# First feed-forward of a two-layer transformer kernel: the inner layers by seven products of quarters instead of eight

## The reference, cut to what matters

```python
x = L0_attn_x                                            # (4, 1024, 256)
x = x + _L0_attn_ref(_layernorm(x), Wq, Wkv_down, Wk_up, Wv_up, Wo)      # 8 heads of 64
x = x + _L0_ffn_ref(_layernorm(x), w1_w, w1_s, w2_w, w2_s, h1_w, h1_s, h2_w, h2_s, w3_w, w3_s)
x = x + _L1_attn_ref(_layernorm(x), wq, wk, wv, wo)      # 16 heads of 16, rotary
x = x + _L1_ffn_ref(_layernorm(x), w_gate, w_up, w_down) # integer weights

def _L0_ffn_ref(x, ...):                                 # the part that is changed
    def _tlin(x, w, s):  return jnp.einsum('bsi,oi->bso', x, w) * s      # w is -1, 0 or 1
    h = silu(_tlin(x, w1_w, w1_s)) * _tlin(x, w2_w, w2_s)                # 256 -> 1024, gate and up
    h = gelu(_tlin(h, h1_w, h1_s))                                       # 1024 -> 1024
    h = gelu(_tlin(h, h2_w, h2_s))                                       # 1024 -> 1024
    return _tlin(h, w3_w, w3_s)                                          # 1024 -> 256
```

## Time and profile before

| | |
|---|---|
| Median of three executions | 2337.16 us (2336.05 to 2341.58) |
| The profiled execution, its own time | 2332.85 us |
| Its span, first to last instruction | 2331.0 us |
| TensorE busy | 2286.6 us, 98% |
| VectorE, ScalarE, GpSimd busy | 1378.5, 1463.2, 1001.8 us |
| Mean granted TensorE clock | 0.996 |

### The profile page before, as it was taken

How to read it: one execution, slowest core, us unless ns; L and a number is a source line. 1 busy time by engine, 2 the same in 40 slices (tenths; PEclk the granted TensorE clock), 3 DMA queues, 4 the chain that set the end, 5 groups by cost and what they waited for, 6 DMA issues and landing times.

```text
span 2331.0 us, 39372 instructions
## 1 busy us (share of the span) xinstructions
PE 2286.6 (98%) x14921; PEld 1414.8 (61%) x14921; DVE 1378.5 (59%) x2150; ACT 1463.2 (63%) x2049; POOL 1001.8 (43%) x646
## 2 busy tenths in 40 slices
PE   7999999999998999999999999999999999999999
PEld 5455555555556888888888886444444444444688
DVE  6655766666743143232232224889889889998364
ACT  5777777777764444444444443678777777778643
POOL 2676766757763373664655645120100000000354
PEclk9999999999999999999999999999999999999999
DMA  2213222222214455555555546343332332331232
GB/s 63 69 52 100 82 74 84 82 80 76 74 31 165 158 178 183 183 182 192 182 175 190 193 165 190 92 105 77 90 87 59 93 82 64 92 90 41 81 112 77
DMA packets 156841, 259.07 MB, mean 111 GB/s; under 512 B 37004, under 2 KB 97292, under 8 KB 156300
## 3 DMA queue, kind: packets, MB, share of 16 engines
q1 hardware_dynamic: 156652, 256.53, 36.6%
HBM read 206.52 MB, written 60.68 MB: 115 GB/s over the span
## 4 chain that ended last, share of the span: by engine, by line
PE 63%; ACT 2%; DVE 1%; issue 1%; DMA 1%; SPq 1%; POOL 0%; POOLq 0%
PE m_R L130 47%; PE m_O L130 11%; PE m_X L130 4%; ACT m_P L1813 1%; DMA m_K<-bounce_k 1%; PE m_X L227 1%; SPq L1671 0%; DVE m_mraw L1965 0%; ACT m_OS L1820 0%; PE m_X L2179 0%; DVE m_ln_x L206 0%; PE m_R L227 0%; DMA inverses<-m_rinv 0%; DVE m_ln_stat L184 0%; SPq L1698 0%
## 5 line engine op out<-in xcount | busy, mean ns | idle before, releaser
L1965 DVE TENSOR_REDUCE m_mraw<-m_R 128x2 f32<-128x1024 f32 x512 | 622.6, 1221 | 68.5 <-PE m_R L130 56.0
L1813 ACT ACTIVATE m_P<-m_R 128x1024 f32<-128x1024 f32 x512 | 523.7, 1025 | 148.6 <-PE m_R L130 148.3
L130 PE MATMUL m_O<-m_P,m_V 128*17 128x256 f32 x4096 | 329.4, 393 | 4.4 <-ACT m_P L1813 2.5
L785 DVE CUSTOM_DVE_ANT_0 a_excess<-a_X,a_excess 128x512 f32<-128x512 f32 x256 | 166.5, 688 | 170.6 <-PE a_X L130 167.9
L955 POOL TENSOR_TENSOR a_accp<-a_accp,a_P 128x1024 f32<-128x1024 f32 x96 | 253.9, 2645 | 24.5 <-ACT a_P L631 16.2
L631 ACT ACTIVATE a_P<-a_S 128x1024 f32<-128x1024 f32 x256 | 249.7, 1040 | 8.5 <-PE a_S L130 8.5
L2070 POOL TENSOR_TENSOR m_act0l<-m_xf,m_act0h 128x512 fp32r<-128x512 f32 x128 | 164.8, 1290 | 209.2 <-ACT m_xf L1875 110.9
L130 PE MATMUL m_R<-m_act0h,wt 128*128 128x512 f32 x640 | 251.4, 393 | 0.0
L130 PE MATMUL m_R<-m_act0l,wt 128*128 128x512 f32 x640 | 250.4, 391 | 0.0
L130 PE MATMUL a_O<-a_P,a_V 128*64 128x512 f32 x1024 | 247.7, 605 | 0.0
L130 PE MATMUL m_R<-m_Q,m_K 64*128 64x512 f32 x800 | 200.1, 497 | 2.3 <-DVE m_mraw L1965 2.0
(11 more groups left out here) (274 smaller groups left out, 4130.1 us busy)
## 6 DMA issues: line engine op xcount, KB each, us to landing
wt<-wcopy SPq DMA_DIRECT2D x176, 512.0 KB, 3.3
m_K<-bounce_k SPq DMA_DIRECT2D x96, 128.0 KB, 5.5
m_ln_x<-x SPq DMA_DIRECT2D x23, 512.0 KB, 4.0
a_tile<-in_L_ffn_tiles SPq DMA_DIRECT2D x22, 512.0 KB, 3.6
wcopy<-in_L_ffn_tiles SPq DMA_DIRECT2D x22, 512.0 KB, 5.0
x<-xres SPq DMA_DIRECT2D x78, 128.0 KB, 1.7
m_Q<-bounce_q SPq DMA_DIRECT2D x150, 64.0 KB, 2.3
xres<-x SPq DMA_DIRECT2D x64, 128.0 KB, 2.7
```

What stands on the lines that cost most here:

```text
L130: return pe.eng.matmul(out, lhsT, rhs, start=start, stop=stop, skip_group_check=True)
L785: dve.eng.tensor_tensor_reduce(excess[:, h, :], bank(key), excess[:, h, :], 1.0, LOWEST, ALU.add, ALU.max, mraw[u % 2][:, q, h:h + 1]).the ...
L1813: act.eng.activation(P[h % 4][:, :, :], pair(key)[:, :, :], ACT.Exp, scale=SCALE).then_inc(R.free(key))
L1965: dve.eng.tensor_reduce(mraw[u % 2][:, at, :], pair(key)[:, :, :], AX.X, ALU.max).then_inc(R.free(key))
```

## The change

Two blocks of 512 tokens still belong to one sequence, and they are now worked on together: a round is 128 slots of five products. For each of the hidden layers and each block pair, the 1024x1024 weight matrix and the 1024x1024 activations (features by the tokens of both blocks) are cut into quarters, and the product is made from seven products of quarters, m1 to m7 (`ORDER`), where eight were made before. Of the seven weights three are quarters as they are, and four are sums and differences of quarters; of the seven activation operands three are quarters (b11, b21, b22) and four are sums and differences (t1 to t4). Gate, up and down are as before. A round has 640 products: 128 for gate and up, 224 for each hidden layer, 64 for down; two blocks of the kernel before have 704.

What goes with it:

- **Mixed weights, in `attention_a`.** Between the 22nd tile's compare and the last feed-forward's tiles lie 32 turns for four groups (`mix_at`, `mix_moves`, `mix`). A group makes four mixed tiles: SyncE loads quarters into `tile` and `tile_hi`, VectorE adds or subtracts them (128x1024), SyncE stores the outcome to `wcopy` (now 38 tiles). SyncE's steps 0, 2, 4 and 6 of a group are at the end of turns with j = 2, 0, 2, 0, VectorE's steps 1, 3, 5, 7 at the end of turns with j = 3, 1, 3, 1. To make room, the first 22 tiles take three turns each, so that their compares fall on every j; those of the last five are at j=2. The rounded tile is now written as int8.
- **Mixed activations, in the feed-forward.** VectorE makes them with four chained additions or subtractions for each of four tiles of a layer (`mix`, 16 instructions of 128x512 with both inputs in SBUF). VectorE also takes m3 to m7 out of PSUM with an addition (`leave`, 20 a layer); ScalarE keeps m1 aside, and does Gelu in place in SBUF (`gelu`).
- **High and low parts** are made for each operand of each product (`high` on ScalarE, `low`). GpSimd makes the low parts of b11, b21, d11 and d21, VectorE all others: b22, t1 to t4, d22, d12.
- **Side work** is done for the block two before, and has new slots: in an even half of a round C_STATS 21, C_SCALE 24, C_TURN 28 and 30, PROJECT from 32 on. The side work of the last two blocks comes after START. The norm of block 1 is done in the first slots (2, 4, 7, 9).
- **Second attention:** the 24 early maxima are one in two slots from slot 456 on (`FIRST_MAX`), through one pair of banks. `m_V`, `m_P`, `m_ON`, `m_K1` and others hold feed-forward values until the end, so their fills are done late, on GpSimd (`fill_late`), five memsets ahead of the first load of V.

The diff, cut to its core (`...` marks what is left out):

```diff
-    LOWS0, LOWS, LOW_FIRST = 22, 27, 6
+    LOWS0, LOWS, LOW_FIRST = 22, 27, 4
+    MIXES, MIX_STEPS = 4, 8
+    MIX_FIRST = LOW_FIRST + 3 * LOWS0
+    LAST_FIRST = MIX_FIRST + MIXES * MIX_STEPS + 1
...
+            def load_quarter(n, to, row, col):
+                buffer = (tile, tile_hi)[to]
+                sp.eng.dma_start(f32(buffer[:, :]) if to else buffer[:, :], quarter(n, row, col)).then_inc(s_quarter[to], 16)
+
+            def store_mix(n, which):
+                layer, mp = divmod(n, 2)
+                sp.wait_ge(s_mix, 4 * n + (1, 2, 4, 3)[which])
+                sp.eng.dma_start(wcopy[LOWS0 + 8 * layer + 2 * which + mp], tile[:, :]).then_inc(s_mixed, 16)
+
+            def mix_moves(n, step):
+                if step == 0:
+                    sp.wait_ge(s_low, LOWS0)
+                    if n:
+                        store_mix(n - 1, 2)
+                    if n < MIXES:
+                        load_quarter(n, 1, 1, 1)
+                        sp.wait_ge(s_mixed, 64 * n)
+                        load_quarter(n, 0, 1, 0)
+                elif step == 2:
+                    store_mix(n, 0)
+                    load_quarter(n, 1, 0, 0)
+                elif step == 4:
+                    store_mix(n, 1)
+                    load_quarter(n, 1, 0, 1)
+                elif step == 6:
+                    store_mix(n, 3)
+                    load_quarter(n, 1, 0, 0)
+                    sp.wait_ge(s_mixed, 64 * n + 48)
+                    load_quarter(n, 0, 1, 0)
...
+            def mix(n, step):
+                first, second = tile[:, :], f32(tile_hi[:, :])
+                dve.wait_ge(s_quarter[0], 16 * (2 * n + (1 if step < 7 else 2)))
+                dve.wait_ge(s_quarter[1], 16 * (4 * n + (step + 1) // 2))
+                if step == 1:
+                    dve.eng.tensor_tensor(first, first, second, ALU.add).then_inc(s_mix)
...
+                elif step == 5:
+                    dve.wait_ge(s_mixed, 64 * n + 32)
+                    dve.wait_ge(s_mix, 4 * n + 2)
+                    dve.eng.tensor_tensor(first, second, first, ALU.subtract).then_inc(s_mix)
...
-    NB, MT, PER, SLOTS = 8, HID0 // 128, 22, 64
+    NB, MT, PER, SLOTS, PACE = 8, HID0 // 128, 40, 64, 5
...
+    ORDER = ("m1", "m2", "m6", "m7", "m4", "m5", "m3")
+    OPERAND = dict(zip(ORDER, ("b11", "b21", "t2", "t3", "t4", "t1", "b22")))
...
-    C_LOAD, C_STATS, C_SCALE, C_TURN = 10, 15, 18, (22, 24)
+    C_LOAD, C_STATS, C_SCALE, C_TURN = (16, 10), (21, 15), (24, 18), ((28, 30), (22, 24))
...
+    def by_pool(op):
+        return op[0] in ("b11", "b21", "d11", "d21")
...
+            def mix(l, j):
+                x11, x12, x21, x22 = [whole[place][j] for place in ("11", "12", "21", "22")]
+                n = 4 * mix_order[l, j]
...
+                dve.eng.tensor_tensor(x22, x22, x12, ALU.subtract).then_inc(s_mixed)
+                dve.wait_ge(s_mixed, n + 1)
...
+                dve.eng.tensor_tensor(x12, x12, x11, ALU.subtract).then_inc(s_mixed)
+                dve.wait_ge(s_mixed, n + 2)
+                dve.eng.tensor_tensor(x11, x22, x11, ALU.add).then_inc(s_mixed)
+                dve.wait_ge(s_mixed, n + 3)
...
+                dve.eng.tensor_tensor(x21, x21, x11, ALU.subtract).then_inc(s_mixed)
+
+            def low(op):
+                dve.wait_ge(*high_done(op))
+                hi, lo = operand(op)
+                dve.eng.tensor_tensor(lo, in_place(op), f32(hi), ALU.subtract).then_inc(s_lo[0])
...
                 for key in ended_at(H):
                     if key[0] == "up":
                         up(key)
+                    elif key[0] in ("m6", "m7", "m4", "m5", "m3"):
+                        leave(key)
+                for op in lows_at(H, False):
+                    low(op)
+                for l, j in mixes_at(H):
+                    mix(l, j)
```

572 lines of the change are left out of this document (406 added, 166 removed).

## The result

The changed kernel takes **2424.85 us** (median of four executions, 2423.22 to 2426.65), the kernel before beside it 2337.75: ratio **1.037**, 95% interval 1.0352 to 1.0388. It is 87 us slower; the forecast was 17 slower, and the range ended at 2382. The profiled execution has a span of 2424.9 us and a mean granted clock of 0.975 (before 0.996).

What follows compares the result with a forecast made beforehand. TensorE, with work for 98% of the span, was taken as the bound. -58.1 + 32 + 4 + 27 + 10 + 2 = +17 on the profiled 2332.9 gave 2349.8, as a median 2354 us; range 2302 to 2382.

Steps and rivals of the forecast that it cites:

- the 4 us of the compares: First attention: compares now fall on every j, eleven of 27 on j=2, where TensorE already waits; +4 us (0 to 11).
- at the same pitch: TensorE: 256 fewer matmuls, each at 0.227 us as before, worth -58.1 us.
- 32 + 4: First attention: +32 us from VectorE's waits for quarters (16 to 48), +4 us from compares on other turns.
- 27 + 10: Feed-forward: TensorE waits for VectorE's chain, +27 us in even halves (22 to 36), +10 us in odd halves (0 to 16).
- those of the 7: Feed-forward, last round's odd half: six maxima lie in VectorE's stretch and the first is waited for at once; +7 us.
- step 0 to 1: First attention: a store must land before the quarter's load; VectorE waits 7.0 us three times, 3.4 in the first group.
- step 4 to 5: First attention: store and load issued at 0.4 us each, landing 3.6 us later; VectorE waits 3.4 us, four times.
- 0.7 us of each wait is covered: First attention: TensorE wants a bank some 0.7 us after the maximum is normally done; 8 x 0.7 off 38 us.
- the 1.34 us of idle time are used up by the mix: First attention: VectorE's 1.34 us idle before the next maximum goes to the 1.22 us mix, so waits reach TensorE nearly whole.
- a second block's side work after START: Second attention: part of the small items, with block 1's norm and five late memsets; together +2 us (0 to 8).
- The first three: Rivals: only quarters' loads cost, 2317 us, 0.14; only the feed-forward costs, 2322 us, 0.10; both hidden, 2285 us, 0.10.
- The fourth: Rival, feed-forward: GpSimd's instructions stand in the way of VectorE's; +24, 2378 us, chance 0.18.

Runs made afterwards that it cites:

- e10: The changed kernel with its tile and mixing schedule one turn later and SyncE's stores and loads of quarters at the start of its turn: 2375.8 us.
- e14: e10 with each of the feed-forward's 128 operand-mix additions working on 8 of 512 columns: 2337.4 us.
- e3: The kernel before with 40 unused VectorE reductions of 128x1024 added, five at a time in eight turns (j=3): 2390.1 us.
- e4: The kernel before with 40 unused VectorE reductions of 128x1024 added, two at a time in twenty turns (j=0 and j=2): 2342.8 us.
- e8: The changed kernel with its tile and mixing schedule one turn later and VectorE making every low part of the feed-forward, GpSimd none: 2390.4 us.
- e15: e10 with even halves' turns and projections later, residual tiles loaded earlier, and GpSimd doing half of the even halves' operand mixes: 2378.6 us.

## Why the prediction was wrong in size

**Right.** 256 products less. SyncE behind its inverses, eight waits at L898 and L906 in the turns named, VectorE's chain in the even halves at 21.2 for 22.3 us, TensorE waiting for `next_lo` and `m_ln_x` there (for `next_lo` 3.8, 3.4 and 5.0 us, where 5 and more was forecast), and what the first attention loses without the mixing at 5.5 for the 4 us of the compares. The mechanism of the forecast is the one that happened, and e10 and e14 each take one half of it away.

**The term that was missing: the clock.** This is the step that failed most. Each step was costed as idle time of TensorE, and the work behind a stall was taken to run as before ("at the same pitch"), without a reason: the sum had no term for it. 49.5 us of the result are work that ran longer: 21.2 in the first attention, 28.3 after it, 10.6 of these tied to the operand mixes by e14. e3 shows the same without any part of the change. This is 49.5 of the 77 us by which the spans' difference (94) missed the sum (+17).

**The idle time was too small in every stage.** The other 27.6 us are TensorE's idle time, 102.6 for a forecast of 75: 45.7 for 32 + 4 in the first attention, 45.4 for 27 + 10 in the feed-forward, 11.5 for 2 behind START. In the feed-forward the sum came nearer than its terms: 19.8 us at the places of the 27, 4.4 at those of the 7, and the rest in waits the forecast did not name; it is in part luck that 37 stands so near 45.

**The term that was too small: the loads of quarters.** The steps at 3.4 and 7.0 us gave 38; the waits were 48.1. The long ones of step 0 to 1 were met, 25.7 us (5.1, 8.0, 5.2, 7.5) for 3.4 + 3 x 7.0 = 24.4. The short ones of step 4 to 5 were not, 22.4 us (4.5 to 6.5) for 4 x 3.4 = 13.6: SyncE's store and load took 1.0 us to issue where one 0.4 was counted, and the load, with a store just ahead of it, was waited for 4.9 to 5.4 us from its issue, where the landing was taken at 3.6 from the earlier trace rows. The 4.9 that the prediction reads there as a store "beside another transfer" is a copy from DRAM to DRAM; the stores of the mixes landed in 3.3. The next step, "0.7 us of each wait is covered", was wrong the other way: e3 shows 1.8 us for each pause, e4 2.1. And "the 1.34 us of idle time are used up by the mix" must then be counted on the other side, as VectorE's work: 48.1 + 8 x 1.22 - 8 x 1.8 = 43.5, an estimate, against 45.7 us of idle time found, some 4 of them the compares'.

**The term for what is small:** "a second block's side work after START", +2. The work itself cost nothing in the sum, 15 us moved from one full stage to another. The stage has 11.5 us more of idle time, and 8 us of clock with it: waits for m_K 5.7 us where they were 1.0, for maxima 5.2 for 2.0, for xres 2.9 for none. Of this only the wait for xres was taken away by an experiment; what makes m_K late was not settled, and in e4, with the code of before, it is 3.2.

**The rivals.** The first three fell with the waits. The fourth, GpSimd in the way of VectorE, fell by its own condition, mixes and low parts at 1.0 us or more in the mean. The mixes took 0.69, as GpSimd has nearly nothing in those slots; VectorE's low parts took 0.83 in the mean and 1.05 in one group of 32, so the mechanism is there in part, some 27 us of VectorE over the stage, and e8, which lessens it, gained no time. e15 shows it in full as soon as GpSimd works beside the mixes.
